# Expert token lists built from half tiles of 64 tokens instead of tiles of 128, in an attention and mixture-of-experts layer

## What is computed

```
e = topk_idx.reshape(-1)                       # token-major, 8 experts per token
oh = jax.nn.one_hot(e, E, dtype=jnp.int32)
pos = jnp.take_along_axis(jnp.cumsum(oh, 0) - 1, e[:, None], 1)[:, 0]
valid = pos < CAP                              # CAP = 256, E = 64
buf = jnp.zeros((E, CAP + 1, h)).at[e, pos_c].set(x[token])[:, :CAP]
```

## Time and profile before

| | us |
|---|---|
| median of 3 runs | 1312.73 (1310.9 to 1312.99) |
| time of the profiled execution | 1313.61 |
| its span in the trace | 1311.9 |
| count step on TensorE (389.82 to 466.49) | 76.67 |
| slots step on TensorE (466.49 to 553.01) | 86.52 |

### The profile page before, as it was taken

How to read it: one execution, slowest core, us unless ns; L and a number is a source line. 1 busy time by engine, 2 the same in 40 slices (tenths; PEclk the granted TensorE clock), 3 DMA queues, 4 the chain that set the end, 5 groups by cost and what they waited for, 6 DMA issues and landing times.

```text
span 1311.9 us, 27512 instructions
## 1 busy us (share of the span) xinstructions
PE 1285.5 (98%) x9478; PEld 1131.3 (86%) x9478; DVE 954.0 (73%) x2431; ACT 556.4 (42%) x1139; POOL 505.6 (39%) x405
## 2 busy tenths in 40 slices
PE   7999999999999999999999999999999999999999
PEld 6788888888888887799898898998988989989987
DVE  6987978888896659957667577676785776767844
ACT  6566556555653433333333333333333333333322
POOL 2110100110010039637356366274573653745710
PEclk8999999999999999999999999999999999999999
DMA  7565535363442212157576486575774756656755
GB/s 239 178 241 189 176 113 174 101 193 118 153 166 70 81 49 81 34 166 165 126 168 172 99 196 138 129 170 128 171 171 107 194 130 159 165 125 160 173 175 194
DMA packets 124919, 194.66 MB, mean 148 GB/s; under 512 B 12016, under 2 KB 98608, under 8 KB 124592
## 3 DMA queue, kind: packets, MB, share of 16 engines
q1 hardware_dynamic: 94384, 147.99, 34.7%
q0 software_dynamic: 30464, 45.83, 19.1%
HBM read 148.62 MB, written 57.74 MB: 157 GB/s over the span
## 4 chain that ended last, share of the span: by engine, by line
PE 80%; DVE 12%; issue 3%; DMA 2%; POOL 1%; ACT 1%; SPq 0%; DVEq 0%; ACTq 0%; POOLq 0%
PE bank L719 21%; PE bank L802 7%; PE bank L769 7%; PE bank L852 7%; PE bank L734 6%; PE bank L820 6%; PE bank L751 5%; PE bank L787 5%; PE bank L861 4%; PE bank L790 4%; PE bank L760 3%; PE bank L842 2%; DVE Dt L1367 2%; DVE At L1388 2%; POOL sel_all L599 1%
## 5 line engine op out<-in xcount | busy, mean ns | idle before, releaser
L575 POOL DMA_INDIRECT acc<-arena,idx_all x128 | 216.5, 1692 | 129.2 <-issue 68.0
L567 POOL DMA_INDIRECT arena<-table,idx_all x132 | 161.0, 1220 | 201.6 <-ACT share L1060 146.6
L719 PE MATMUL bank<-xp,wq 128*128 128x512 f32 x768 | 215.0, 415 | 0.0
L719 PE MATMUL bank<-xp,wk 128*128 128x512 f32 x768 | 203.9, 400 | 0.2 <-DVE wk L1288 0.2
L719 PEld LDWEIGHTS bank<-xp,wk 128*128 128x128 f32 x768 | 141.1, 188 | 34.1 <-DVE wk L1288 0.6
L719 PEld LDWEIGHTS bank<-xp,wq 128*128 128x128 f32 x768 | 141.0, 190 | 28.6 <-issue 0.5
L1367 DVE TENSOR_TENSOR_SCAN Dt<-decay,eye_b 128x512 f32<-128x512 f32 x128 | 158.1, 1236 | 0.6 <-DMA decay<-decay_dram 0.6
L769 PE MATMUL bank<-qT,kT 128*128 128x128 f32 x1024 | 136.2, 276 | 2.5 <-DVE At L1388 2.5
L1040 ACT ACTIVATE qT<-bank 128x512 f32<-128x512 f32 x128 | 76.6, 598 | 133.8 <-PE bank L719 133.8
L769 PEld LDWEIGHTS bank<-qT,kT 128*128 128x128 f32 x1024 | 125.8, 193 | 3.4 <-DVE At L1388 2.8
L802 PEld LDWEIGHTS bank<-V,kw 128*128 128x128 f32 x960 | 117.5, 191 | 11.7 <-issue 9.8
(11 more groups left out here) (160 smaller groups left out, 2262.1 us busy)
## 6 DMA issues: line engine op xcount, KB each, us to landing
decay<-decay_dram SPq DMA_DIRECT2D x64, 512.0 KB, 5.6
carry<-decay_dram SPq DMA_DIRECT2D x60, 512.0 KB, 4.6
arena<-in_L_attn_x_dram SPq DMA_DIRECT2D x16, 512.0 KB, 4.4
table<-arena SPq DMA_DIRECT2D x16, 512.0 KB, 3.7
xT_dram<-arena SPq DMA_DIRECT2D x16, 512.0 KB, 3.0
arena<-in_L_ffn_w_gate_dram SPq DMA_DIRECT2D x64, 128.0 KB
arena<-in_L_ffn_w_up_dram SPq DMA_DIRECT2D x64, 128.0 KB
arena<-in_L_ffn_w_down_dram SPq DMA_DIRECT2D x64, 128.0 KB
```

The costliest lines, as they stand in the source:

```text
L567: pool.indirect_dma_start(out=xg[:, e % 2, j, :], out_offset=None, in_=table[:, :], in_offset=bass.IndirectOffsetOnAxis(ap=idx_all[:, e, j ...
L575: pool.indirect_dma_start(out=acc[:, :], out_offset=bass.IndirectOffsetOnAxis(ap=idx_all[:, e, j:j + 1], axis=0), in_=yb[:, e % 2, j, :], ...
L719: last = mm(to[:, :], w[:, part, k, h * DK:(h + 1) * DK], xp[:, other, k, :], start=(k + i == 0), stop=(k == KD - 1 and i == 2))
```

## The change

A token tile of 128 becomes two half tiles of 64 (`HT`), so that 128 half tiles (`TH`) lie on the partitions where 64 tiles did. In the count step eight experts fill a bank (`CB`), with three products of 64 columns for an expert: two accumulate on partitions 0 to 63 and one goes to 64 to 127. In the slots step four experts fill a bank; the products contract over 128 rows and have 64 columns. GpSimd makes `reach` for two of each four experts and VectorE for the other two. One comparison of the whole bank, one copy and one sum take the place of eight comparisons with sums and two copies. `sel_cur` moves into the shared arena, over the place of `xt`, and is zeroed later; the list constants are built behind the first DMA issues and leave the set that the other engines wait for.

```
-N_CONSTS = 10
+N_CONSTS = 5
+HT = P // 2
+TH = 2 * T
 EB = 4
-
-COUNT_AT = [(s, place) for s in range(2, H + 1) for place in ((1, 2, 3) if s < 4 else (1, 3))]
-assert len(COUNT_AT) == E // EB
-PAIR_AT = [(s, place) for s in range(1, H) for place in ((0, 1, 2, 4, 3) if s in (2, 4, 6) else (0, 1, 2, 3))]
-PAIR_AT += [(H, 0)]
-assert len(PAIR_AT) == E // 2
+CB = 8
+
+COUNT_AT = [(s, 2) for s in range(2, H + 1)] + [(H, 3)]
+assert len(COUNT_AT) == E // CB
+FOUR_AT = [(s, place) for s in range(1, H) for place in ((0, 4, 2) if s == 4 else (0, 2))] + [(H, 0)]
+FOUR_AT.sort(key=lambda at: (at[0], (0, 1, 2, 4, 3).index(at[1])))
+assert len(FOUR_AT) == E // EB
...
-        reach = sel_all[0:T, :, :, :].rearrange("p e b c -> p (e b c)")[:, 0:2 * EB * CAP]
+        sel_cur = view(2, [P, CB * (T + 1)]).bitcast(BF16).rearrange("p (u e t) -> p u e t", u=2, e=CB)
+        reach = sel_all[:, :, :, :].rearrange("p e b c -> p (e b c)")[:, 0:2 * EB * CAP]
         reach = reach.rearrange("p (u e s) -> p u e s", u=2, e=EB)
-        junk = view(2, [P, EB // 2 * NHALF, P])
+        passed = view(2, [P, 2, EB * NHALF * HT // 2]).bitcast(BF16)
...
-            for m in (ident[:, :], upper[:, :], lower[:, :], before[:, :]):
-                pool.memset(m, 1.0).then_inc(w_ident, 1)
+            pool.memset(ident[:, :], 1.0).then_inc(w_ident, 1)
             pool.memset(eye_b[:, :, :], 1.0).then_inc(w_ident, 1)
             zeros = gated[:, 0:XW]
             pool.memset(zeros, 0.0).then_inc(w_ident, 1)
-            pool.wait_ge(w_ident, 6)
+            pool.wait_ge(w_ident, 3)
...
-            pool.memset(ones_t[:, :], 1.0).then_inc(consts, 1)
-            pool.memset(sel_cur[:, :, :, 0:1], 0.0).then_inc(consts, 1)
             pool.memset(zeros_t, 0.0).then_inc(consts, 1)
...
+
+            for m in (upto[:, :], beyond[:, :], second[:, :], before[:, :]):
+                pool.memset(m, 1.0).then_inc(list_ones, 1)
+            pool.memset(ones_t[:, :], 1.0).then_inc(list_consts, 1)
+            pool.wait_ge(list_ones, 4)
...
             pool.wait_ge(zero_rows, 16 * 2 * NHALF)
...
+            pool.wait_ge(xn_stored, 16 * C)
+            pool.wait_ge(xT_ps, 2 * C)
+            pool.memset(sel_cur[:, :, :, 0:1], 0.0).then_inc(sel_zeroed, 1)
             weights_out(C - 1)
...
             def reach_group(g, u):
 
-                wait_past(pool, tok_ps, 2 * (g - 1))
-                for j in range(EB):
+                wait_past(pool, tok_ps, g - 1)
+                for j in range(EB // 2, EB):
                     ins = pool.tensor_scalar(reach[:, u, j, :], slot_row, firsts[:, EB * g + j:EB * g + j + 1], None,
                                              ALU.is_ge)
                 ins.then_inc(reach_ready, 1)
...
@@ -679,29 +698,43 @@
                 wait_past(pe, cnt_cp, g)
                 if g == 0:
                     pe.wait_ge(aT_cp, C)
+                    pe.wait_ge(list_consts, 5)
+
+                def first_half(j, previous):
+                    return mm(bank[7][0:T, j * HT:(j + 1) * HT],
+                              sel_cur[:, g % 2, j, 1 - previous:T + 1 - previous], (upto, beyond)[previous][:, :],
+                              start=(previous == 0), stop=(previous == 1))
+
+                def second_half(j):
+                    return mm(bank[7][T:TH, j * HT:(j + 1) * HT], sel_cur[:, g % 2, j, 1:T + 1], second[:, :],
+                              start=True, stop=True)
+
+                for j in range(0, CB, 2):
+                    first_half(j, 0)
+                    second_half(j)
+                    first_half(j, 1)
+                    second_half(j + 1)
+                    first_half(j + 1, 0)
+                    last = first_half(j + 1, 1)
+                last.then_inc(cnt_ps, 1)
+
+            def first_counts():
+                pe.wait_ge(cnt_cp, E // CB + 1)
+                mm(bank[7][:, 0:E], before[:, :], totals, start=True, stop=True)
+                mm(bank[7][:, E:2 * E], ones_t[:, :], totals, start=True, stop=True).then_inc(first_ps, 1)
+
+            def slots_of_four(q):
+
+                pe.wait_ge(reach_ready, q + 1)
+                pe.wait_ge(reach_dve, q + 1)
+                wait_past(pe, tok_cnt, q - 1)
+                if q == 0:
+                    pe.wait_ge(first_cp, 1)
                 for j in range(EB):
-                    dst = bank[7][0:T, j * P:(j + 1) * P]
-                    mm(dst, sel_cur[:, g % 2, j, 1:T + 1], upper[:, :], start=True, stop=False)
-                    last = mm(dst, sel_cur[:, g % 2, j, 0:T], lower[:, :], start=False, stop=True)
-                last.then_inc(cnt_ps, 1)
-
-            def first_counts():
-                pe.wait_ge(cnt_cp, E // EB + 1)
-                mm(bank[7][0:T, 0:E], before[:, :], totals, start=True, stop=True)
-                mm(bank[7][:, E:2 * E], ones_t[:, :], totals, start=True, stop=True).then_inc(first_ps, 1)
-
-            def slot_pair(n):
-
-                pe.wait_ge(reach_ready, n // 2 + 1)
-                wait_past(pe, tok_cnt, n - 1)
-                if n == 0:
-                    pe.wait_ge(first_cp, 1)
-                for j in range(2):
                     for half in range(NHALF):
-                        lo = (j * NHALF + half) * P
-                        last = mm(expert_bank[n % 2][:, lo:lo + P],
-                                  reach[:, (n // 2) % 2, 2 * (n % 2) + j, half * P:(half + 1) * P],
-                                  rise[:, 2 * n + j, :], start=True, stop=True)
+                        lo = (j * NHALF + half) * HT
+                        last = mm(expert_bank[q % 2][:, lo:lo + HT], reach[:, q % 2, j, half * P:(half + 1) * P],
+                                  rise[:, EB * q + j, :], start=True, stop=True)
                 last.then_inc(tok_ps, 1)
...
             def select_group(g):
                 if g == 0:
+                    act.wait_ge(sel_zeroed, 1)
                     act.wait_ge(sel_kept, C)
                 wait_past(act, cnt_ps, g - 1)
                 act.copy(sel_cur[:, g % 2, :, 1:T + 1],
-                         sel_all[:, g * EB:(g + 1) * EB, :, :].rearrange("p e b c -> p e (b c)"))\
+                         sel_all[:, g * CB:(g + 1) * CB, :, :].rearrange("p e b c -> p e (b c)"))\
                    .then_inc(selc_ready, 1)
...
-                dve.tensor_copy(rise[:, g * EB:(g + 1) * EB, :].rearrange("p e t -> p (e t)"), bank[7][0:T, :])\
+                dve.tensor_copy(rise[:, g * CB:(g + 1) * CB, :].rearrange("p e t -> p (e t)"), bank[7][:, :])\
...
-                tab_link(dve.memset(rise[:, :, P - 1:P], 1.0))
+                tab_link(dve.memset(rise[:, :, HT - 1:HT], 1.0))
                 dve.tensor_copy(sums[:, :], bank[7][:, E:2 * E])
-                tab_link(dve.tensor_copy(firsts, bank[7][0:T, 0:E]))
+                tab_link(dve.tensor_copy(firsts, bank[7][:, 0:E]))
                 dve.nop().then_inc(first_cp, 1)
-
-            def count_pair(n):
-
-                wait_past(dve, tok_cnt, n)
-                dve.wait_ge(tok_ps, n + 1)
-                pair = expert_bank[n % 2]
-                for j in range(2 * NHALF):
-                    half = j % NHALF
-                    ts(junk[:, j, 0:P - 1], pair[:, j * P:j * P + P - 1], slot_col[:, half:half + 1], None,
-                       ALU.is_le, ALU.add, accum_out=cnt[:, 2 * n + j // NHALF, half:half + 1])
-                last_cols = pair[:, :].rearrange("p (e h t) -> p e h t", e=2, h=NHALF)[:, :, :, P - 1]
-                dve.tensor_copy(tiles[:, 2 * n:2 * n + 2, :], last_cols).then_inc(tok_cnt, 1)
+                dve.wait_ge(slot_row_ready, 1)
+                for g in range(2):
+                    reach_half(g)
+
+            def reach_half(g):
+                for j in range(EB // 2):
+                    ins = ts(reach[:, g % 2, j, :], slot_row, firsts[:, EB * g + j:EB * g + j + 1], None, ALU.is_ge)
+                ins.then_inc(reach_dve, 1)
+
+            def count_four(q):
+
+                wait_past(dve, tok_sum, q - 1)
+                dve.wait_ge(tok_ps, q + 1)
+                four = expert_bank[q % 2][:, :].rearrange("p (e h t) -> p e h t", e=EB, h=NHALF)
+                slots = slot_col[:, None, :, None].broadcast_to([P, EB, NHALF, HT - 1])
+                tt(passed[:, q % 2, :, :, 0:HT - 1], four[:, :, :, 0:HT - 1], slots, ALU.is_le).then_inc(tok_passed, 1)
+                dve.tensor_copy(tiles[:, EB * q:EB * (q + 1), :], four[:, :, :, HT - 1]).then_inc(tok_cnt, 1)
+                dve.wait_ge(tok_passed, q + 1)
+                dve.tensor_reduce(cnt[:, EB * q:EB * (q + 1), :], passed[:, q % 2, :, :, 0:HT - 1], AX.X, ALU.add)\
+                    .then_inc(tok_sum, 1)
+                if q + 2 < E // EB:
+                    reach_half(q + 2)
 
```

More of the change, by code:

```diff
@@ L93, in build @@
         eye_b = sb("eye_b", [P, B, P])
[L94 to L97, removed]
+        upto = sb("upto", [P, HT], BF16)
+        beyond = sb("beyond", [P, HT], BF16)
+        second = sb("second", [P, HT], BF16)
```

(42 more changed lines are left out.)

13 lines of the change are left out of this document (7 added, 6 removed).

## The result

The changed kernel takes 1294.62 us (median of 4 runs, 1293.95 to 1294.84) against 1312.86 us before: 18.2 us less, a ratio of 0.986 with an interval of 0.9845 to 0.9874. Faster was forecast, at 1297.2 us with a range of 1292.5 to 1303.5.

The account below looks back on a forecast made before the run. TensorE was taken to bound the count step, three engines in turn the slots step. From 1313.61 us, 4.5 (count) and 11.0 (slots) less gave 1298.1 us profiled, 1297.2 by the median; range 1292.5 to 1303.5.

Parts of the forecast that it names:

- What bounds it: Whole kernel: the slots step is held by TensorE, VectorE and GpSimd in turn, the count step by TensorE alone.
- Fixed cost: TensorE, count and slot groups: 0.28 to 0.30 us where partial-form products begin or end, unless against the outputs.
- Count step: TensorE: 66.2 us of attention plus 6.0 us for eight count groups, 72.2 us in all, 4.5 us less.
- The term p: Count step, TensorE: time of one 64-column count product, taken as 0.029 us, bounds 0.018 and 0.055.
- Slots on TensorE: Slots step: 66.2 us plus 128 products at 0.053 us, priced from a float32 update, no fixed cost: 73.0 us.
- the clock row: Slots step before, TensorE: clock 0.98 read as 2% of 86.5 us, 1.7 us at the lower clock.
- Slots on VectorE: Slots step: 55.0 us of work instead of 65.4, giving 75.8 us; 75.5 us taken, 11.0 us less.
- the density: Slots step, VectorE: busy share behind the first count stays 65.42 / 68.05 = 0.96.
- sentence on `reach`: Slots step, VectorE: by the skill's four bf16 numbers a cycle, rows cost under 0.16 us, step some 1 us shorter.
- GpSimd: Slots step: 32 instead of 64 `reach` rows at 0.914 us, 29.2 us instead of 58.5; it leaves the path.
- Start: Kernel start, fewer constants on GpSimd and zeroing DMAs earlier: costed at 0, bounds -1 to +1 us.
- The slower rival: Slots step: VectorE at half rate for four-dimensional broadcast patterns, slots 98 us, kernel 1320 us; chance 0.05.

Follow-up runs that it names:

- experiment 1: Kernel before, with a pair's four comparisons with running sums made one comparison of the bank and one sum, tiles still 128: 1314.1 us against 1311.57, ratio 1.0019.
- experiment 2: Kernel before, with two of each four rows of `reach` made by VectorE: 1313.59 us, ratio 1.0017.
- experiment 3: Kernel before, with slot products contracting over 128 rows, the upper 64 of `rise` being zero: ratio 0.9999, slots step 85.42 us.
- experiment 4: Changed kernel with all `reach` rows back on GpSimd: 1301.91 us, ratio to before 0.9925, slots step 80.37 us.
- (8): Changed kernel with count groups behind the query projection (place 1 instead of 2), away from the outputs: one execution, 1296.02 us, count step 71.94 us.
- experiment 7: Changed kernel with VectorE's half of `reach` moved to ScalarE as a steep sigmoid: 1290.85 us, ratio to before 0.9844, slots step 70.20 us.
- experiment 6: Changed kernel with count products ordered so that the two halves of the array are not interleaved: 1293.49 us, ratio to before 0.9863, count step 71.86 us.
- experiment 5: Changed kernel with all `reach` rows on VectorE and none on GpSimd: 1297.06 us, ratio to before 0.9901, slots step 77.42 us.

## Why the prediction was right, and what was off

*What bounds it.* Right that three engines held the slots step and TensorE the count step. Experiments 1 to 3 each took one part of the change by itself: +2.5, +2.0 and -0.3 us. None pays alone, and without the split 8.3 of the 14.4 us are missing (4). Only experiment 3 is the relief of one engine and nothing else: the first adds work to VectorE, the second moves work to it. What a relief of VectorE alone would give in the kernel before was not run. A sum over parts that gave each its own saving would have been wrong; the forecast took the larger of two engine sums, and that held.

*Fixed cost.* Right in the main: most of it goes with the form (experiment 3), and groups against the outputs share it (8). In the slot groups all but the 0.07 us at the update is gone, where the forecast had nothing left. The rule of the Trainium skill that the prediction cites (TensorEngine Tiling, Key Properties: a change of the tiling mode drains TensorE) agrees, as far as these three forms go.

*Count step, forecast 72.2, measured 70.82.* The term p was mis-sized: 0.029 forecast, 0.022 measured; 168 x 0.007 = 1.2 us, nearly all of the 1.4. I had a lower bound of 0.018 for full overlap of the halves, and the runs show 0.031 within one half and 0.022 interleaved, close to it.

*Slots on TensorE, forecast 73.0.* The prediction's reading of the clock row is loose: 1.7 us is what a mean of 0.98 costs, not the time at the lower level, which is twice that, the lower level being half (0.50 from 546 to 548 us). The sum needs only the cost. Without waits TensorE takes 70.20 (experiment 7): the 128 slot products cost 0.030, not 0.053, 2.9 us less. The row taken for the price, the float32 update, was the wrong one: a weight load lasts 192 ns there and 98 ns for a slot product, in the median. That the weight load sets the price of either is not shown. The Trainium skill (TensorE: Matmul & The Clock Gate, Weight-path perf modes) says that loads of 128 weights that are not float32 are sped up; that is consistent with 0.030, and the prediction passed it over. But weights of 64 columns, which that rule leaves out, cost 0.031 (experiment 6), so no run here shows that it is the cause. At 0.030 the sum is 66.2 + 3.8 = 70.0, which would not have changed the forecast, since VectorE stood above. In this the forecast was lucky: an error of this size on the engine that bounds the step would have reached the time.

*Slots on VectorE, forecast 75.8, taken 75.5, measured 72.11.* Behind the first count the forecast had 55.0 / 0.96 = 57.3 us, and it was 54.24, 3.1 less. The larger part, 1.8 us, is the density, and this is the step that failed: I divided by 0.96 as if an engine always kept that share of idle time. It was time in which VectorE waited for others, and it goes as soon as VectorE has clearly the most to do: 99.8% in experiment 1, where GpSimd's rows and the number of groups were as before, and 99% in the changed kernel. The other 1.2 us is the work, 53.83 instead of 55.0, in which errors of both signs partly cancel. The 28 rows of `reach` in this stretch took 6.2 us, where 5.1 was forecast for all 32. The groups took 1.30 on average instead of 1.33, 0.5 less. The pairs before had taken 1.19 on average from start to start, not the 1.15 of the one in the earlier trace rows, so that the 28.6 us left for other work was over 1 us too high. And the scans, 1304 ns on average before, took 1217, 0.7 us less; they took 1324 in experiment 4 with GpSimd as busy as before, and 1215 in 5 with GpSimd idle. The prediction's sentence on `reach` by the Trainium skill (VectorE: DVE Perf Modes, The perf-mode tier table) is not borne out: it had a row come out below 0.16, and no row did, the cheapest pairs taking 0.19 to 0.195 a row.

The two steps were forecast 4.8 us too long, the time by the median only 2.6; the parts outside the two steps gave the rest back.

*GpSimd* left the path, but only thanks to the split (4). Its 32 rows took 35.8 us instead of 29.2, which the slack hid. *Start*: costed at 0; no difference beyond the scatter. *The slower rival* needed half rate for the broadcast comparison; it took 0.67 us for 504 numbers, no more than one operation over a bank in the earlier trace rows.

## What to carry to other kernels

Where several engines hold a step at once, add up each engine's work for the changed step and take the largest, without adding the idle time of the old step; a saving on an engine that shares the step with others can be worth next to nothing, as 6.4 us of TensorE were here. Merging small vector instructions pays only if the data of a bank stands for more results: count the numbers read, not the instructions. Small products of a partial form belong against other work of that form, or are better padded to the full one, and what an engine at its limit still does should go to the one with time left.

## What the runs showed that was not expected

Padding half of the contraction with zeros makes a group of four slot products cheaper, 0.32 instead of 0.53 us. A bf16 product of 64 columns costs 0.030 us whether its weights have 64 columns (0.031) or 128 (0.030). And GpSimd and VectorE seem to slow each other's rows of `reach` down. GpSimd's row takes 1.13 us on average in the changed kernel and 1.15 in experiment 2, where VectorE makes its own beside it, and 0.925 in experiment 7, where it makes none; in the kernel before and in experiment 4, where it makes none either but GpSimd makes all 64, it is 1.02 to 1.03. VectorE's row lasts at most 288 ns with GpSimd idle (experiment 5) and up to 523 in the changed kernel. What they would share is not shown.
